# Head roots times layer scale as a TensorE matrix, and x added by a DMA from GpSimd, in an mLSTM cross-attention and MX feed-forward kernel

## What is computed

```python
# per head, 16 heads of 32 columns
D = jnp.exp(log_D - max_log_D)
C = qk * D                                   # qk scaled by 1/sqrt(32)
Cn = C / (jnp.maximum(jnp.abs(C.sum(-1, keepdims=True)), jnp.exp(-max_log_D)) + EPS)
h = jnp.einsum('bhst,bhtd->bhsd', Cn, vh)
hn = (h - mu) * jax.lax.rsqrt(var + EPS)
hn = hn * ln_scale.reshape(1, nh, 1, dh)     # layer scale, 512 values
...
x = x + attention(_layernorm(x), ctx, ctx, ...)
x = x + ffn(_layernorm(x), w_gate, w_up, w_down)   # operands rounded to block formats
```

## Time and profile before

| what | us |
|---|---|
| median of 3 runs | 553.61 (552.74 to 558.61) |
| the profiled execution | 553.07, of which its span is 551.3 |
| PE, DVE, ACT, POOL busy in the span | 454.0, 432.6, 244.9, 245.2 |
| stage 1, to the first `c_mult` | 0 to 107.1 |
| stage 2, to the last step's first `c_mult` (b = 7) | 107.1 to 313.3 |
| last step and start of the feed-forward | 313.3 to 376.5 |
| feed-forward in its steady pace and its end | 376.5 to 551.3 |

### The profile page before, as it was taken

How to read it: one execution, slowest core, us unless ns; L and a number is a source line. 1 busy time by engine, 2 the same in 40 slices (tenths; PEclk the granted TensorE clock), 3 DMA queues, 4 the chain that set the end, 5 groups by cost and what they waited for, 6 DMA issues and landing times.

```text
span 551.3 us, 10415 instructions
## 1 busy us (share of the span) xinstructions
PE 454.0 (82%) x3465; PEld 300.7 (55%) x3465; DVE 432.6 (78%) x615; ACT 244.9 (44%) x343; POOL 245.2 (44%) x231
## 2 busy tenths in 40 slices
PE   0597795599789696969788785399999999999984
PEld 0497795287657484757566562144444444444441
DVE  3769888478797897978787965997788788788880
ACT  2466664247264353545364544234434344344341
POOL 2444531323635536273736563543454443443433
PEclk9767886589859586776859697899999999999996
DMA  6655621412321414050421101201111111112111
GB/s 164 214 173 175 224 97 38 137 54 85 134 62 60 137 42 144 11 173 22 134 62 55 42 26 52 77 0 40 38 38 53 61 38 38 38 38 75 39 38 39
DMA packets 30564, 43.70 MB, mean 79 GB/s; under 512 B 6980, under 2 KB 11972, under 8 KB 30532
## 3 DMA queue, kind: packets, MB, share of 16 engines
q1 hardware_dynamic: 30532, 43.26, 24.3%
HBM read 34.41 MB, written 8.85 MB: 78 GB/s over the span
## 4 chain that ended last, share of the span: by engine, by line
PE 42%; issue 20%; POOL 17%; DVE 13%; ACT 4%; DMA 3%; POOLq 1%; SPq 1%; DVEq 0%; ACTq 0%
PE psA L1335 9%; PE psC L1362 9%; PE psA L1344 9%; PE psB L1354 3%; POOL wq L559 3%; POOL early L616 3%; PE psA L1234 2%; PE psC L1214 2%; DMA early<-in_x_dram 2%; POOL xc L649 2%; DVE wy L952 2%; DVE wq L955 1%; POOL qs L644 1%; PE psC L1173 1%; POOL rs L553 1%
## 5 line engine op out<-in xcount | busy, mean ns | idle before, releaser
L679 POOL TENSOR_TENSOR kTa<-kTa,ps 128x1024 bf16<-128x1024 bf16 x32 | 61.2, 1912 | 102.7 <-DVE kTa L1116 102.7
L1262 PE MATMUL psA<-vp,DC 128*128 128x128 f32 x512 | 73.7, 312 | 2.1 <-DVE DC L1019 2.1
L559 POOL TENSOR_TENSOR wq<-wq,ws 128x1024 bf16<-128x1024 bf16 x24 | 50.6, 2108 | 54.9 <-DVE wq L955 54.9
L1262 PEld LDWEIGHTS psA<-vp,DC 128*128 128x128 f32 x512 | 71.4, 227 | 4.0 <-issue 4.0
L1335 PE MATMUL psA<-WgT,qTa 128*128 128x512 bf16 x256 | 63.7, 394 | 7.5 <-ACT hf L813 3.9
L1362 PE MATMUL psC<-WdT,kTa 128*128 128x512 bf16 x256 | 62.2, 387 | 2.4 <-ACT kTa L879 2.4
L1344 PE MATMUL psA<-WuT,qTa 128*128 128x512 bf16 x256 | 61.3, 383 | 0.0
L879 ACT ACTIVATE kTa<-psB 128x1024 bf16<-128x1024 bf16 x32 | 32.8, 1024 | 54.5 <-PE psB L1354 54.2
L1019 DVE SCALAR_TENSOR_TENSOR DC<-psA,DC 128x512 f32<-128x512 f32 x64 | 41.7, 686 | 15.7 <-PE psA L1234 8.3
L1104 DVE TENSOR_TENSOR kTa<-kTa,psA 128x1024 f32<-128x1024 f32 x32 | 39.0, 1220 | 18.2 <-PE psA L1344 18.2
L804 ACT ACTIVATE DC<-psB 128x512 f32<-128x512 f32 x64 | 37.6, 597 | 23.6 <-PE psB L1248 23.2
(11 more groups left out here) (131 smaller groups left out, 849.7 us busy)
## 6 DMA issues: line engine op xcount, KB each, us to landing
early<-in_x_dram SPq DMA_DIRECT2D x16, 512.0 KB, 4.1
early<-in_ctx_dram SPq DMA_DIRECT2D x8, 512.0 KB, 4.6
wraw<-in_L_ffn_w_down_dram SPq DMA_DIRECT2D x8, 512.0 KB, 5.5
wraw<-in_L_ffn_w_gate_dram SPq DMA_DIRECT2D x8, 512.0 KB, 4.2
wraw<-in_L_ffn_w_up_dram SPq DMA_DIRECT2D x8, 512.0 KB, 3.6
x_scratch<-early SPq DMA_DIRECT2D x8, 512.0 KB, 3.0
kTa<-x_scratch SPq DMA_DIRECT2D x16, 256.0 KB, 2.7
out_dram<-kTa SPq DMA_DIRECT2D x16, 256.0 KB, 2.0
```

Source lines behind the costliest of these rows:

```text
L559: nc.gpsimd.tensor_tensor(blocks(wq[p][:, :]), blocks(wq[p][:, :]), spread(ws4[p][:, :], UB), ALU.mult).then_inc(wq_ready.sem, 1)
L679: nc.gpsimd.tensor_tensor(blocks(pd[h]), blocks(pc[h]), spread(ps4[h][:, :], PB), ALU.mult).then_inc(pq_ready.sem, 1)
L1262: last = nc.tensor.matmul(psA[:, j, to:to + P], DC[n % DCN][:, i4 * P:(i4 + 1) * P], values[:, left:left + P], start=i4 == 0, stop=c == 0, ...
```

## The change

- **Roots and layer scale.** `ltab` [32 x 512] holds the layer scale of head h in row h and zeros elsewhere (two selections on POOL, once). For each batch PE transposes the roots (`root_transpose`, two transposes into `psC[1]`), ACT copies them to `rT` (`copy_root`), and PE multiplies `rT` by `ltab` (`scale_root`, one f32 matmul of 32 x 512 for each half, into `psC[1]` and `psC[0]`). `head_norm` becomes two DVE instructions of 512 columns: `hf` times that PSUM matrix, written straight into `x1`.
- **x by DMA.** `residual` is now `gp.dma_start(x1, x_v[b], accum_op=ALU.add)` on POOL's queue; `load_xr`, `xr`, `lns` and both POOL instructions are gone. `x1_stats` and `store_x1` wait for `x_added`.
- **Orders of stage 2** are changed on every engine: on ACT `x1_norm(b-1)` moves from ahead of `copy_h(b, 1)` to behind `exps(b+1, 3)`, and `evac_gate_up` moves back; on PE both `w_transpose` move back and `x_transpose` comes behind the scale matmuls; on POOL `w_back` comes ahead of `residual` and `weigh` ahead of the second `w_back`; on DVE `w_pow` moves between the two `head_norm` halves and `x1_stats` behind the second `w_front`.
- **Stage 1:** constants are loaded from ACT's queue, `tables` comes after the second `x_rsqrt`, the last but one `w_transpose` of `w_down` comes after the gates, `d_ld` is split by buffer and half, and `qk(0, 0)` is issued before the decays.
- **Start of the feed-forward:** the rounding of batches 6 and 7 and the finish of batch 7 are spread, in pieces, between the pairs of tiles 0 to 6. The last roots are taken with POOL's power (`last_power`), 16 columns for each half, in place of ACT's logarithm and exponential.

```diff
@@ pe, step @@
             def step(b, p, n, first, last):
-                w_transpose(2 * b + B, 0, rows_order)
                 for k in range(HPC):
                     heads(b, p, k)
                 decay(b, p, 4)
                 decay(b, p, 5)
+                w_transpose(2 * b + B, 0, rows_order)
                 centre(b, 1)
                 qk(b, 1)
-                if b >= 2:
+                if not first:
                     pe.wait_ge(wT_ev.sem, wT_ev.unit(2 * b + B))
-                    x_transpose(b - 2)
+                    root_transpose(b - 1)
                 state(b)
+                if not first:
+                    scale_root(b - 1, 0, 1)
                 decay(b, p, 6)
                 decay(b, p, 7)
+                if not first:
+                    pe.wait_ge(state_ev.sem, state_ev.at(b, 1))
+                    scale_root(b - 1, 1, 0)
+                    pe.wait_ge(hn_ready.sem, hn_ready.at(b - 1, 1))
+                if b >= 2:
+                    x_transpose(b - 2)
                 for k in range(HPC, 2 * HPC):
                     heads(b, p, k)
                 inter(b, p)
+                if not last:
+                    decay_qk(b + 1, 1 - p)
...
+                    centre(b + 1, 0)
+                    decay(b + 1, 1 - p, 2)
+                    decay(b + 1, 1 - p, 3)
                 if b >= 2:
                     pe.wait_ge(xqT_ev.sem, xqT_ev.at(b - 2, 1))
                 w_transpose(2 * b + B + 1, 1, rows_order)
@@ vector @@
+            def head_norm(b, p, c, bank):
+
+                ve.wait_ge(r_mm.sem, r_mm.at(b, c + 1))
...
+                nc.vector.tensor_tensor(x1[:, c].rearrange("p (h d) -> p h d", d=DH), hf[p][:, c, :, 0:DH],
+                                        psC[bank][:, :].rearrange("p (h d) -> p h d", d=DH),
                                         ALU.mult).then_inc(hn_ready.sem, 1)
@@ gpsimd @@
             def residual(b):
...
+                gp.wait_ge(hn_ready.sem, hn_ready.at(b, 2))
                 settle(gp)
-                nc.gpsimd.tensor_tensor(x1, hn, xr, ALU.add).then_inc(x1_ready.sem, 1)
+                gp.dma_start(x1, x_v[b], accum_op=ALU.add).then_inc(x_added, 16)
@@ scalar, step @@
                 if not last:
                     round_const(2 * b + B + 2, 0)
-                if not first:
-                    x1_norm(b - 1)
                 copy_h(b, p, 1)
-                evac_gate_up(2 * b + B + 1, 1, b)
                 if not last:
                     exps(b + 1, 0)
                     exps(b + 1, 1)
                     copy_v(b + 1, 1 - p, 0)
                     exps(b + 1, 2)
                     exps(b + 1, 3)
+                if not first:
+                    x1_norm(b - 1)
+                evac_gate_up(2 * b + B + 1, 1, b)
                 square(b, p)
```

303 lines of the change are left out of this document (191 added, 112 removed).

## The result

The changed kernel takes 585.41 us (median of 4 runs, 583.37 to 586.02) against 553.17 for the kernel before in the same comparison: ratio 1.0633, 95% interval 1.0596 to 1.0670. It is slower by 32 us; the profiled execution has a span of 581.7 us against 551.3, so +30.4 inside the span. In what follows, a run that lay over 1.5% above the fastest of its kernel is left out of the ratios but not of the medians (e1, e2, e8, e11 and e13 have one each), and the profiled executions of e8 and e11 are such runs, so of e11's trace only orders and waits are read, and e8's period may be too long.

A forecast was written before the change was run, and what follows sets the result against it. Bound: a chain that changes engine, neither DVE nor PE being full. Entry -4.2, six periods +11.1, last step +4.6, feed-forward -4.2 make +7.3 on 553.07: 560.4, with 0.5 for the median 561 us; range 546 to 577.

The forecast's parts named there:

- F to Z: Stage 2, from a step's fifth c_mult (F) to the next step's first (Z): 17.35 us after, against 17.9.
- Priced at full clock, since PE now works on without a gap: Behind a step's fifth c_mult: heads and inter through at 5.7 us, last exps at 11.3, all at full clock.
- The DMA: Adding x in each step: taken as 5 us, hidden in all steps but the last; x may come at 7.7.
- Z to F: Stage 2, from a step's first c_mult (Z) to its fifth (F): 15.1 us after, against 12.7.
- The period: One step of stage 2: 32.4 us after, against 30.59, so +1.85.
- the clock rises late: Rival in stage 2: clock rises some 12 us after PE starts, not 4; period 35.4, 582 us; chance 0.13.
- the clock is kept: Rival in stage 2: PE's 7 us gap doesn't lower the clock; period 30.85, 550 us; chance 0.18.
- Six periods: The six whole periods of stage 2 from step 1 to step 7: +11.1 us together.
- the last step: Last step of stage 2, first c_mult to fifth: 10.5 us before, 15.1 after, +4.6.
- entry: Way into stage 2: earlier loads, qk and w_transpose off the way to the first heads; -4.2 us.
- Start of the feed-forward: From the last step's fifth c_mult through the pairs: -6.1 or -2.4 us, the middle, -4.2, taken.
- DVE has 0.9 to spare in a half, so 2 to 2.5 us show: Feed-forward behind pair (2, 0): of some 8 us of pieces between pairs, only 2 to 2.5 show.

The follow-up runs named there:

- e1: Changed kernel with ScalarE running x1_norm(b-1) between exps(b+1, 1) and copy_v(b+1, 0) instead of behind exps(b+1, 3); 587.0 us, ratio 1.057.
- e2: Changed kernel with 20 filler matmuls, results never read, behind w_transpose where TensorE idles; 576.0 us, ratio 1.041.
- e8: Changed kernel with next batch's c_mult and w_pow ahead of x1_round, copy_h ahead of head_power, x1_round(B-2) back in the last step; 573.3 us.
- e11: Kernel before with only the root matrix added, all orders kept, x added by GpSimd from a buffer; 563.9 us, ratio 1.020.
- e13: e1 with GpSimd's w_back ahead of weigh instead of behind it; 583.6 us, ratio 1.049.
- e12: e2 with the same 20 filler matmuls a second time, ahead of state(b); 605.2 us, ratio 1.096.
- e14: Changed kernel with x1_norm ahead of copy_v, w_back ahead of weigh, filler in TensorE's idle time, x1_round(B-2) back in the last step; 568.4 us.
- e3: Changed kernel without the accumulating DMA: x is loaded by SP into its own buffer and added by GpSimd; 581.9 us, ratio 1.053.
- e6: Changed kernel with x1_round(B-2) and back_x(B-2) in the last step again, ahead of the first pair; 583.1 us, ratio 1.055.
- e7: Kernel before with the accumulating DMA in place of GpSimd's addition, no root matrix, all orders kept; 568.8 us, ratio 1.030.
- e4: Changed kernel with VectorE running the four c_mult(b+1, 0..3) and w_pow ahead of x1_round(b-1); 581.3 us, ratio 1.050.
- e10: Kernel before with c_mult(b+1, 0..3) and w_pow ahead of x1_round, and head_power behind copy_v(b, p, 1); 578.1 us, ratio 1.049.

## Why the prediction was wrong

Forecast were 561 us, slower, in a range to 577; measured 585. The direction and the chain were right, and the loss was four times the size. The step that failed most is the clock of `heads` 4 to 7.

- **F to Z** (17.35 forecast, 19.7 measured): the mechanism was as written, `x1_norm` right behind the last `exps`, `x1_round` behind it, `c_mult` and PE queued behind that, Z 4.4 us after its start (forecast 4.5). The step that failed is "Priced at full clock, since PE now works on without a gap". `heads` took 6.46 and not 3.8, so `x1_norm` started at F + 13.75 and not 11.3. PE did work without a gap, and the clock fell anyway. Where e12 kept the clock, the same sum came out: the last `exps` ended at F + 11.2, and F to Z was 17.7 to 18.0. That the stretch would be bound at about 18 us even at full clock, by the DMA's way, was missed too (e12, e14): POOL's root was priced at 1.95 us, and `nm` to `nb` takes 3.25. Two small instructions take 0.93 and 1.20 for 0.19 each beside DVE's `w_round`, with which they end:

```profile
219.55 1.19 DVE L985 SCALAR_TENSOR_TENSOR wy<-wy,wm 128x1024 f32<-128x1024 f32 x1
220.77 1.22 DVE L988 SCALAR_TENSOR_TENSOR wq<-wy,wm 128x1024 bf16<-128x1024 f32 x1
```

- **The DMA**: 5.7 us (median from issue to landing) against 5 taken. `x1_stats` did wait, 1.4 us, which the text had named as what would be wrong; but as it said, x could come late at no cost as long as `x1_norm` waits for `exps`, and e3 beside e6 confirms it. The condition for that cover was an order of this change: without it the DMA costs 3% (e7).
- **Z to F** (15.1 forecast, 14.44 measured): right. `scale_root` 1.12, `root_transpose` 0.39 for 0.3, `copy_root` 0.37 for 0.4, PE's gap 6.77 for 7, `heads` 5.20 for 5.6, with the clock up 2.9 us into them (forecast 3.8). To some degree that is luck: in e6, the same code in these steps, the split was 15.5 and 18.6, with 6.3 us for `heads` 0 to 3 and 5.4 for 4 to 7.
- **The period**: +1.85 forecast; by landmarks +3.56. Of this 0.8 is structure and 2.75 clock, by e12's period at full clock. The rival that the clock rises late (582) had the nearest number by the wrong half: `heads` 0 to 3 behaved as forecast, and the loss is at F, where no case had a fall. The rival that the clock is kept (550) did not come about, and the filler that keeps it in the first half (e2) shows that it is a cost one can take back in part.
- **Six periods** +23.0 for +11.1; the last step +3.95 for +4.6; entry -2.9 for -4.2, where scatter between executions is larger than either.
- **Start of the feed-forward** (-4.2 forecast with all that follows, +6.4 measured, -2.0 and +8.4): the first pair came at F + 17.75, forecast 17.3. `last_power` took 2.90 and 3.34 us, between the bounds and near the upper one, and ended at F + 37.2 (forecast 32.4 or 36); with a whole `gate` between `root_transpose` and `scale_root` on PE, DVE's `head_norm` waited 5.07 us behind it, and pair (2, 0) came at F + 50.7 where 44.3 to 47.9 was forecast. The second step that failed is "DVE has 0.9 to spare in a half, so 2 to 2.5 us show". The pieces behind pair (2, 0) are 10.4 us, not 8, and 8.4 of them show (4.5 for the 4.4 above; e6: 3.6 back for `x1_round(6)` alone). A pair is a link in the chain from `up` through pair and `back_p` to the next transposes, so what stands between two pairs delays PE too; the wait of 1.71 for PE above shows it in one place, and no run tests it further. A share of idle time is not slack: that was read from busy time where it had to be read from the chain.
- **Why the kernel before is not held up by its low clock**: its granted clock is lower, and PE runs at 1.2 GHz for more than half of the period (a mean of 0.72 between 1.00 and 0.50). This part is read from one trace and tested by no run. DVE has `w_front`, `w_round` and `x1_round` in hand meanwhile and the only idle time of over 0.4 us that its timeline shows in that period is the 2.25 for POOL. The change puts PE on DVE's way twice a period, for the scale matrix and behind `exps`, and there the clock costs time.

Of the 30.4 us, then, some 16.5 (6 x 2.75) are the clock, 5 the structure of the period (6 x 0.8), 1.6 the first period, which is longer than the others, 4 the last step, 8.4 the pieces, less 2.9 and 2.0. The split of the period rests on a kernel with filler and is an estimate from those two kernels.

## What to carry to other kernels

Before moving work from POOL or DVE onto TensorE, look which engine waits for which: while TensorE was off the chain here, its half clock cost little, and once it was on it, the same clock had a price, also behind work without a gap. Here a wait taken away was mostly given back elsewhere, by the clock, an instruction held up by another engine or the next engine's order, so a repair is to be judged by the period and not by the wait that went (e1, e4, e13). Work put between the links of a loop that runs at its bound showed nearly whole; ahead of the loop, where an engine idles, a part of it was free (e6), though not after every other edit (e8).

## What the runs showed of the hardware

- The granted clock fell to 0.50 with TensorE busy and no gap over 0.13 us (211 us in the changed kernel), and within a gap of 1.28 us (e2) where it had survived one of 2.26. The Trainium skill, page TensorE: Matmul & The Clock Gate, tells in section HAM oscillation of falls in idle gaps, and in section A second HAM failure mode of falls with small gaps between groups of matmuls. The first fits 227.9 and e10 (gaps of 6.77 and 6.80 us); for the fall at 211 the trace shows no such gaps.
- VectorE and GpSimd hold each other up in both directions: 0.18 us became 1.83 (e1, L967), and on GpSimd 0.19 became 1.20 (L539, beside `w_round`, in the changed kernel).
- A DMA issued by GpSimd that adds 512 KB from HBM onto SBUF: 5.7 us median from issue to landing, 1.28 us of GpSimd. The plain load of the same size was 4.1 us and 3.5 in the changed kernel.
- GpSimd's power on 16 columns takes 2.90 and 3.34 us, on 2 columns mostly 0.7, in single cases up to 1.96.
